# The first three score rows of the next batch, computed in pieces beside the second attention

## The chip, the cores and the metric

One Trainium2 chip, one core of it. The metric is the device time of one execution in microseconds (us); the kernel works on 8 batches one after the other.

## What is computed

The reference, cut to its steps. A batch is 128 channels by 48 x 48 = 2304 positions ("tokens"). All of it is float32.

```
x = x + _L0_conv_ref(_gn(x), ...)          # group norm, then:
#   q, k, v = W x + b;  energy = q^T k  (2304 x 2304);  attn = softmax(energy, rows)
#   gamma * (v attn^T) + x * sigmoid(se_w2 relu(se_w1 mean(x)))
t = _to_tokens(x)
t = t + _L1_attn_ref(_ln_t(t))             # softmax(s s^T) s over 2304 tokens, s = layer norm of t
t = t + _L1_ffn_ref(_ln_t(t), ...)         # 8 experts, the best 2 of each token by router softmax
x = _from_tokens(t, x)
```

## The kernel before

There are no loops on the chip: a list of steps, `PLAN`, is written out, and every engine walks it in order and issues its own part of each step. A step is a tuple such as `("scores", b, n, r, c)`. Each engine is therefore an in-order queue, and semaphores join the queues. Every product is made of three single-pass matmuls of a high and a low part (function `three`, lines 1022 to 1024), so each tensor that goes into one is split first: ScalarE writes the high part, VectorE subtracts it for the low part.

A batch has two attentions.

- **First attention.** It goes in blocks `n` = 0 to 5 of 3 rows of tiles (3 x 128 queries). A stage has 18 slots. In the slots of stage `n`, the scores of block `n` are made (`scores`, 5 chunks for a row: four of 512 columns, one of 256, in PSUM banks 0 to 4), VectorE takes each chunk's maximum (line 840) and the row's (`row_max`, line 844), and ScalarE makes the exponentials into `p_rows` (line 619); the next row's chunks use the same banks, so they wait for these exponentials. In the same slots block `n` - 1 is transposed in 18 pieces (`pt`, line 1036; high part line 631, low part line 850) and multiplied with v (`pv`, into bank 5). Stage 0 has scores alone and stage 6 has `pt` and `pv` of block 5 alone.
- **Second attention.** It has 54 windows `w`. In each, TensorE makes `s1` (six matmuls of 384 columns, banks 0 to 3) and `pv1` of the window two before (six matmuls, banks 4 and 5), ScalarE makes the exponential (line 666) and the high part (line 675), and VectorE the low part (`p1low`, line 924).

Other work is laid beside these windows by tables of window numbers: the statistics, normalisation and q, k, v projections of the next batch (`STATISTICS_SLOTS`, `NORMALISE_SLOTS`, `PROJECT_SLOTS`), the transposes back of the second attention's result (`o1t`, with `o1add`, lines 930 to 938), and the mixture of experts in blocks of 3 tiles (`MOE_SLOTS`, function `moe`): layer norm (`uln`, `uapply`, line 901), transpose (`ut`), `router`, six half products (`expert` for VectorE, line 1005; `scaled` for ScalarE, line 700), GpSimd's sums (lines 519 to 526), and the transpose back `yt`. Of the steps beside a window those named in `SOON` stand ahead of `p1low`. Blocks 4 and 5 of a batch's experts are done beside the second attention of the next batch.

Small results go through a ring of two PSUM banks (6 and 7): each ring step waits until the readers of the step two before have finished (`wait_ring`). Stage 0 of the next batch begins in slots `end` = 54 and up, right behind the last window, beside the last two `pv1`. I call these 18 slots **the turn**; there are seven turns in an execution.

## Time and profile before

| | |
|---|---|
| time, median of 3 runs | 2816.06 us (2815.02 to 2817.49) |
| the profiled execution's own time | 2816.04 us |
| its span in the trace | 2814.3 us |
| TensorE, busy share of the span | 94% |
| VectorE | 77% |
| ScalarE | 72% |
| GpSimd | 16% |

The span runs from the first to the last instruction of the trace; 1.7 us of the profiled time lie outside it. TensorE's busy time is a union of matmuls that overlap and whose ends are modelled, so a busy TensorE is not at its peak, and an idle time that the trace shows before a matmul is a real wait. The granted clock of TensorE is a column of its own.

### The profile page before, as it was taken

Reading aid. Unit: us, or ns where it says so; the run is one execution under the profiler, and the core shown is the slowest. Engines: PE = TensorE matmul, PEld = TensorE weight load, DVE = VectorE, ACT = ScalarE, POOL = GpSimd, SP = SyncE. Lnnn points to the kernel's source line nnn. Section 1 sums busy time; section 2 is a strip of 40 time slices with the busy share of each in tenths; the row PEclk is TensorE's granted clock in tenths of the full one; section 3 lists DMA queues with packets and bytes.
Section 4 is the critical chain, followed back from the end, with each engine's and each line's share of the span. In section 5 each row is a group of like instructions: output and inputs, shape, how many; then the busy total and the mean of one; then the engine's idle time right before and its main releaser. Section 6 shows DMA issues by size and latency. Waiting matters only on the chain.

```text
span 2814.3 us, 45757 instructions
## 1 busy us (share of the span) xinstructions
PE 2638.2 (94%) x15334; PEld 2379.7 (85%) x15334; DVE 2161.1 (77%) x5496; ACT 2027.1 (72%) x4308; POOL 447.5 (16%) x840
## 2 busy tenths in 40 slices
PE   6999999999999999999999999998999999999996
PEld 5889978899788997889888898888988889888895
DVE  6877778777787777877778777787778877788675
ACT  4768767687676876767767687776877778677774
POOL 0000310032101320012300123001220022200223
PEclk9999999999999999999999999999999999999997
DMA  1000000000000000000000000000000000000000
GB/s 36 1 18 1 7 7 1 18 7 9 4 1 18 7 10 4 1 18 7 12 1 1 18 10 9 1 1 21 7 9 1 1 21 7 9 1 1 4 9 12
DMA packets 11320, 23.15 MB, mean 8 GB/s; under 512 B 1360, under 2 KB 7760, under 8 KB 11088
## 3 DMA queue, kind: packets, MB, share of 16 engines
q1 hardware_dynamic: 11088, 20.20, 2.0%
q8 instruction: 127, 2.08, 0.3%
q14 instruction: 105, 0.86, 0.1%
...
## 4 chain that ended last, share of the span: by engine, by line
PE 62%; DVE 23%; ACT 9%; issue 5%; POOL 1%; DMA 0%; ACTq 0%; DVEq 0%; SPq 0%; POOLq 0%
PE ps L1022 18%; PE ps L1024 17%; PE ps L1023 17%; PE ps L1036 9%; DVE mx L840 6%; DVE pt_lo L850 3%; DVE pt_lo L924 3%; ACT pt_hi L631 2%; ACT p_rows L619 2%; DVE u_tok L901 1%; ACT p_rows L666 1%; POOL u_rs L529 1%; ACT pt_hi L675 1%; DVE acc L1005 1%; DVE negmax L844 1%
## 5 line engine op out<-in xcount | busy, mean ns | idle before, releaser
L631 ACT ACTIVATE pt_hi<-ps 128x384 fp32r<-128x384 f32 x864 | 426.3, 493 | 319.4 <-PE ps L1036 314.1
L850 DVE TENSOR_TENSOR pt_lo<-ps,pt_hi 128x384 fp32r<-128x384 f32 x864 | 479.3, 556 | 179.6 <-ACT pt_hi L631 171.6
L619 ACT ACTIVATE p_rows<-ps,negmax 128x512 f32<-128x512 f32 (+1 forms) x720 | 465.5, 648 | 67.2 <-DVE negmax L844 60.4
L924 DVE TENSOR_TENSOR pt_lo<-p_rows,pt_hi 128x768 fp32r<-128x768 f32 x432 | 413.7, 959 | 123.8 <-ACT pt_hi L675 122.0
L840 DVE TENSOR_REDUCE mx<-ps 128x1 f32<-128x512 f32 (+1 forms) x720 | 443.0, 633 | 72.2 <-PE ps L1024 48.5
L1036 PE MATMUL ps<-ident,p_rows 128*128 128x128 f32 x2736 | 456.2, 276 | 43.0 <-DVE pt_lo L850 22.8
L666 ACT ACTIVATE p_rows<-ps,shift 128x768 f32<-128x768 f32 x432 | 389.8, 902 | 118.2 <-PE ps L1024 113.7
L1036 PEld LDWEIGHTS ps<-ident,p_rows 128*128 128x128 f32 x2736 | 331.3, 140 | 159.6 <-issue 60.9
L675 ACT ACTIVATE pt_hi<-p_rows 128x768 fp32r<-128x768 f32 x432 | 365.6, 846 | 39.8 <-PE ps L1024 0.4
L1022 PE MATMUL ps<-pt_hi,v_hi 128*128 128x384 f32 x864 | 358.3, 415 | 2.5 <-ACT y_out L640 2.5
L1022 PE MATMUL ps<-xt_hi 128*128 128x384 f32 x864 | 305.3, 353 | 0.0
L1022 PE MATMUL ps<-pt_hi,tn_hi 128*128 128x384 f32 x864 | 291.8, 338 | 9.6 <-ACT y_out L640 7.6
L1022 PE MATMUL ps<-k_hi,q_hi 128*128 128x512 f32 (+1 forms) x720 | 278.4, 387 | 16.3 <-ACT p_rows L619 16.2
L1024 PE MATMUL ps<-xt_hi,xt_lo 128*128 128x384 f32 x864 | 291.6, 337 | 0.0
L1024 PE MATMUL ps<-pt_hi,v_lo 128*128 128x384 f32 x864 | 291.5, 337 | 0.0
L1023 PE MATMUL ps<-xt_lo,xt_hi 128*128 128x384 f32 x864 | 291.4, 337 | 0.0
L1023 PE MATMUL ps<-pt_lo,v_hi 128*128 128x384 f32 x864 | 290.1, 336 | 0.0
L1024 PE MATMUL ps<-pt_hi,tn_lo 128*128 128x384 f32 x864 | 289.3, 335 | 0.0
L1023 PE MATMUL ps<-pt_lo,tn_hi 128*128 128x384 f32 x864 | 288.9, 334 | 0.0
L1023 PE MATMUL ps<-k_lo,q_hi 128*128 128x512 f32 (+1 forms) x720 | 272.9, 379 | 0.0
L1024 PE MATMUL ps<-k_hi,q_lo 128*128 128x512 f32 (+1 forms) x720 | 271.8, 377 | 0.0
L513 POOL TENSOR_TENSOR ln_rs<-ln_ve,minus_half 128x3 f32<-128x3 f32 x48 | 41.9, 873 | 1302.4 <-DVE ln_ve L888 1302.4
(165 smaller groups left out, 5159.5 us busy)
## 6 DMA issues: line engine op xcount, KB each, us to landing
...
biases<-channel SPq DMA_DIRECT2D x1, 2.0 KB, 4.9
```

Source lines behind the costliest of these rows:

```text
L513: pool.tensor_tensor(ln_rs[:, :], ln_ve[:, :], minus_half[:, :], ALU.pow).then_inc(ln_rstd_ready, 1)
L619: act.activation(p_rows[:, ROW_BUFFER[r, n % 2], a:a + w], ps[:, c, 0:w], ACT.Exp, bias=negmax[:, r % 2:r % 2 + 1], accum_out=dparts[:, n, ...
L631: act.activation(pt_hi[:, slot, :], ring_bank(step)[:, 0:BW], ACT.Copy)\
L666: act.activation(p1_f[:, w % 2, :].rearrange("p (s w) -> p s w", s=2), ps[:, 2 * (w % 2):2 * (w % 2) + 2, 0:BW], ACT.Exp, bias=shift[:, :])\
L675: act.activation(p1_hi[:, w % 3, :], p1_f[:, w % 2, :], ACT.Copy).then_inc(p1_hi_ready, 1)
L840: link(dve.tensor_reduce(mx[:, c:c + 1], ps[:, c, 0:QC[c][1]], AX.X, ALU.max))
L850: dve.tensor_tensor(pt_lo[:, slot, :], ring_bank(step)[:, 0:BW], pt_hi[:, slot, :], ALU.subtract).then_inc(pt_lo_ready, 1)
L924: dve.tensor_tensor(p1_lo[:, w % 3, :], p1_f[:, w % 2, :], p1_hi[:, w % 3, :], ALU.subtract).then_inc(p1_lo_ready, 1)
L1022: pe.matmul(out, lhs_hi, rhs_hi, start=start, stop=False)
L1023: pe.matmul(out, lhs_hi, rhs_lo, start=False, stop=False)
L1024: return pe.matmul(out, lhs_lo, rhs_hi, start=False, stop=stop)
L1036: ins = pe.transpose(ring_bank(step)[:, k * 128:(k + 1) * 128], src(k), ident[:, :])
```

## The change

The scores of block 0 of the next batch (its first three rows, 15 chunks) are no longer made in the turn. They become 15 steps `early`, each in the ring, beside windows 25 to 47 of the second attention. TensorE fills a ring bank with a chunk, ScalarE copies it to `p_rows` in SBUF, VectorE takes its maximum from there (`early`), then the maximum of the row (`early_max`), and ScalarE takes the exponential in place in three pieces of 768 columns (`early_exp`, windows 30 to 53). The turn then starts with stage 1: the scores of block 1 together with `pt` and `pv` of block 0.

With it come: `ROW_BUFFER` and the places of `o1_chan` and `terms` in `p_rows` are exchanged, so that these rows are free; the k, q and v projections, the statistics and the normalisation move to earlier windows; the experts' tables move up, so that the last `yt` stands in window 54 and not 60, each `yt` two windows behind its last `scaled` and no longer three; `uln` and `uapply` of block 4 move into stage 6 of the next batch; and `router` is divided: its last exponential on ScalarE and the operations of VectorE behind it are a step `gates`, one window later.

```diff
-ROW_BUFFER = {(0, 0): 0, (0, 1): 1, (1, 0): 2, (1, 1): 3, (2, 0): 4, (2, 1): 4}
+ROW_BUFFER = {(0, 0): 1, (0, 1): 0, (1, 0): 3, (1, 1): 2, (2, 0): 4, (2, 1): 4}
...
-    if n + 1 < NB and j == 13:
+    if n + 1 < NB and j == 13 and (n or not b):
...
-    if k < 3 and 1 <= row <= NB * TPB:
+    if k < 3 and (TPB + 1 if b else 1) <= row <= NB * TPB:
         s.append(("exp", b, (row - 1) // TPB, (row - 1) % TPB, k + 2))
+    if n == NB and b:
+        s += {7: [("uln", b - 1, 4)], 13: [("uapply", b - 1, 4)]}.get(j, [])
...
-MOE_SLOTS = [(2, 4, range(6, 12), 14), (10, 12, range(15, 21), 23), (21, 23, range(26, 32), 34), (30, 32, range(35, 41), 43),
-             (39, 41, range(44, 50), 52), (47, 49, [52, 53, 54, 55, 56, 57], 60)]
-STATISTICS_SLOTS = [4, 5, 6, 7, 8, 9, 10, 11, 12, 13, 14, 15]
-NORMALISE_SLOTS = [14, 15, 16]
-PROJECT_SLOTS = {15: [("xg", 0)], 16: [("xg", 1)], 17: [("kproj", 0), ("xg", 2)], 19: [("kproj", 1)], 21: [("kproj", 2)],
-                 22: [("kproj", 3)], 23: [("base", 0)], 24: [("kproj", 4)], 25: [("kproj", 5)], 26: [("base", 1)],
-                 28: [("vproj", 0)], 29: [("base", 2)], 31: [("vproj", 1)], 32: [("vproj", 2)], 33: [("vproj", 3)],
-                 41: [("vproj", 4)], 42: [("vproj", 5)], 43: [("qproj", 0)]}
+MOE_SLOTS = [(None, 0, 2, range(4, 10), 11), (6, 10, 11, range(13, 19), 20), (21, 23, 24, range(26, 32), 33),
+             (30, 32, 33, range(35, 41), 42), (39, 41, 42, [43, 44, 44, 45, 45, 46], 48), (44, 47, 48, [50, 50, 51, 51, 52, 52], 54)]
+STATISTICS_SLOTS = [0, 0, 2, 2, 4, 4, 5, 6, 7, 8, 9, 12]
+NORMALISE_SLOTS = [8, 9, 11]
+PROJECT_SLOTS = {10: [("xg", 0)], 11: [("xg", 1)], 12: [("kproj", 0)], 13: [("xg", 2), ("kproj", 1)],
+                 14: [("kproj", 2)], 15: [("kproj", 3)], 16: [("kproj", 4)], 17: [("kproj", 5)], 18: [("qproj", 0), ("base", 0)],
+                 19: [("vproj", 0)], 21: [("vproj", 1)], 22: [("vproj", 2), ("base", 1)], 23: [("vproj", 3)], 24: [("vproj", 4)],
+                 30: [("vproj", 5)], 34: [("base", 2)], 53: [("qproj", 1)]}
+EARLY_SLOTS = [([25, 25, 26, 27, 28], 29, [30, 32, 33]), ([31, 32, 34, 34, 35], 36, [39, 41, 42]),
+               ([39, 40, 43, 46, 47], 48, [49, 51, 53])]
...
+def early(b):
+    s = {}
+    for r, (banks, top, exps) in enumerate(EARLY_SLOTS):
+        for c, slot in enumerate(banks):
+            merge(s, {slot: [("early", b, r, c)]})
+        merge(s, {top: [("early_max", b, r)]})
+        for u, slot in enumerate(exps):
+            merge(s, {slot: [("early_exp", b, r, u)]})
+    return s
...
-SOON = ("expert", "scaled", "kproj", "vproj", "qproj")
+SOON = ("expert", "scaled", "kproj", "vproj", "qproj", "early", "early_max", "gates")
...
-    s = [step for n in range(1, NB + 1) for j in range(NT) for step in attention0(b, n, j)]
+    s = [step for n in range(2 if b else 1, NB + 1) for j in range(NT) for step in attention0(b, n, j)]
...
-        merge(beside, {end + 3: [("o1t", b, 4)], end + 6: [("o1t", b, 5)]})
-        merge(beside, {end + j: attention0(b + 1, 0, j) for j in range(NT)})
-        for m, slot in ((4, end + 4), (5, end + 10)):
-            at = beside[slot].index(("row_max", b + 1, 0, m - 4)) + 1
-            beside[slot].insert(at, ("o1add", b, m))
+        merge(beside, early(b + 1))
+    if b + 1 < B:
+        merge(beside, {end + j: attention0(b + 1, 1, j) for j in range(NT)})
+        merge(beside, {end + 4: [("o1t", b, 4), ("o1add", b, 4)], end + 7: [("o1t", b, 5), ("o1add", b, 5)]})
...
-        o1_chan = p_rows[:, 3, 0:2 * LW].rearrange("p (s w) -> p s w", s=2)
+        o1_chan = [p_rows[:, 2, 0:LW], p_rows[:, 0, 2 * LW:3 * LW]]
...
+                elif kind == "early":
+                    r, c = step[2:]
+                    a, w = QC[c]
+                    act.wait_ge(ring_full, filled(step))
+                    if r == TPB - 1:
+                        act.wait_ge(xg_lo_ready, at(xg_lo_ready, "xg", b, LB - 1))
+                    act.activation(p_rows[:, ROW_BUFFER[r, 0], a:a + w], ring_bank(step)[:, 0:w], ACT.Copy).then_inc(early_copied, 1)
+                elif kind == "early_exp":
+                    r, u = step[2:]
+                    act.wait_ge(early_copied, at(early_copied, "early", b, r, len(QC) - 1))
+                    act.wait_ge(early_max_ready, at(early_max_ready, "early_max", b, r))
+                    row = p_rows[:, ROW_BUFFER[r, 0], u * LW:(u + 1) * LW]
+                    act.activation(row, row, ACT.Exp, bias=early_negmax[:, r:r + 1],
+                                   accum_out=dparts[:, 0, r, u:u + 1]).then_inc(early_exp_ready, 1)
...
-                        act.wait_ge(pv1_done, at(pv1_done, "pv1", b - 1, LB * NT - 1))
+                        act.wait_ge(pv1_done, at(pv1_done, "pv1", b - 1, LB * NT - 3 + j // 2))
...
+                elif kind == "early":
+                    r, c = step[2:]
+                    a, w = QC[c]
+                    dve.wait_ge(early_copied, at(early_copied, *step))
+                    if r and not c:
+                        dve.wait_ge(early_max_ready, at(early_max_ready, "early_max", b, r - 1))
+                    dve.tensor_reduce(early_mx[:, c:c + 1], p_rows[:, ROW_BUFFER[r, 0], a:a + w], AX.X, ALU.max)\
+                        .then_inc(early_ready, 1)
+                elif kind == "early_max":
+                    r = step[2]
+                    dve.wait_ge(early_ready, at(early_ready, "early", b, r, len(QC) - 1))
+                    dve.tensor_reduce(early_negmax[:, r:r + 1], early_mx[:, :], AX.X, ALU.max, negate=True)\
+                        .then_inc(early_max_ready, 1)
                 elif kind == "row_max":
...
+                elif kind == "early":
+                    r, c = step[2:]
+                    if not r and not c:
+                        pe.wait_ge(q_lo_ready, at(q_lo_ready, "qproj", b, 0))
+                        pe.wait_ge(k_lo_ready, at(k_lo_ready, "kproj", b, NB - 1))
+                    wait_ring(step)
+                    a, w = QC[c]
+                    tile = slice(r * 128, (r + 1) * 128)
+                    three(ring_bank(step)[:, 0:w], q_hi[:, 0, tile], q_lo[:, 0, tile], k_hi[:, a:a + w], k_lo[:, a:a + w])\
+                        .then_inc(ring_full, 1)
...
+                    if b and not n:
+                        pe.wait_ge(early_exp_ready, at(early_exp_ready, "early_exp", b, TPB - 1, j // (LW // 128)))
+                    else:
+                        pe.wait_ge(p_rows_ready, at(p_rows_ready, "exp", b, n, TPB - 1, chunk_of(j)))
...
                     link(dve.tensor_scalar(rank[:, :, :], rank[:, :, :], 2.0, None, ALU.is_lt))
-                    dve.wait_ge(vector_chain, chained(step, links[0]))
+                elif kind == "gates":
+                    m = step[2]
+                    shape = [128, TPB, E]
+                    dve.wait_ge(vector_chain, chained(("router", b, m), linked(("router", b, m))))
                     dve.wait_ge(gate_exp_ready, at(gate_exp_ready, *step))
                     link(dve.tensor_tensor(gexp[:, :, :], gexp[:, :, :], rank[:, :, :], ALU.mult))
                     dve.wait_ge(vector_chain, chained(step, links[0]))
```

What it does to the order, at three places of the first batch's end. First TensorE around the turn, before (`ident,acc` is `yt`, `ident,p_rows` in this place `o1t` of the second attention's result, `k_hi,q_hi` scores of block 0):

```order
L1024 MATMUL ps<-ew_hi,u_lo 128x512
L1036 MATMUL ps<-ident,p_rows 128x128 x3
L1022 MATMUL ps<-k_hi,q_hi 128x512
L1023 MATMUL ps<-k_lo,q_hi 128x512
L1024 MATMUL ps<-k_hi,q_lo 128x512
L1022 MATMUL ps<-k_hi,q_hi 128x256
L1023 MATMUL ps<-k_lo,q_hi 128x256
L1024 MATMUL ps<-k_hi,q_lo 128x256
L1036 MATMUL ps<-ident,acc 128x128 x3
L1036 MATMUL ps<-ident,p_rows 128x128 x3
L1022 MATMUL ps<-k_hi,q_hi 128x512
```

The same place after (`ident,p_rows` is now `pt` of block 0, `k_hi,q_hi` scores of block 1, `pt_hi,tn_hi` the last `pv1`):

```order
L1091 MATMUL ps<-ident,acc 128x128 x3
L1091 MATMUL ps<-ident,p_rows 128x128 x3
L1077 MATMUL ps<-k_hi,q_hi 128x512
L1078 MATMUL ps<-k_lo,q_hi 128x512
L1079 MATMUL ps<-k_hi,q_lo 128x512
L1077 MATMUL ps<-pt_hi,tn_hi 128x384
L1078 MATMUL ps<-pt_lo,tn_hi 128x384
L1079 MATMUL ps<-pt_hi,tn_lo 128x384
L1077 MATMUL ps<-pt_hi,tn_hi 128x384
L1078 MATMUL ps<-pt_lo,tn_hi 128x384
L1079 MATMUL ps<-pt_hi,tn_lo 128x384
L1091 MATMUL ps<-ident,p_rows 128x128 x3
```

The experts' products and block 0's scores are gone from the turn, `yt` has moved ahead of the first scores, and a transpose stands beside each chunk. Then ScalarE late in the second attention, before (L666 and L675 are a window's two operations, L700 a `scaled`, L686 the high part of `ut`):

```order
L666 ACTIVATE p_rows<-ps,shift 128x768
L675 ACTIVATE pt_hi<-p_rows 128x768
L700 ACTIVATE p_rows<-ps,gates 128x128 x4
L666 ACTIVATE p_rows<-ps,shift 128x768
L675 ACTIVATE pt_hi<-p_rows 128x768
L666 ACTIVATE p_rows<-ps,shift 128x768
L675 ACTIVATE pt_hi<-p_rows 128x768
L700 ACTIVATE p_rows<-ps,gates 128x128 x4
L686 ACTIVATE u_hi<-ps,plus_one 128x384
```

And after, about the same windows (L700 and L709 are the window's two, L734 a `scaled`, L648 the copy of an `early`, L720 `ut`):

```order
L700 ACTIVATE p_rows<-ps,shift 128x768
L709 ACTIVATE pt_hi<-p_rows 128x768
L734 ACTIVATE p_rows<-ps,gates 128x128 x4
L700 ACTIVATE p_rows<-ps,shift 128x768
L709 ACTIVATE pt_hi<-p_rows 128x768
L734 ACTIVATE p_rows<-ps,gates 128x128 x4
L648 ACTIVATE p_rows<-ps 128x512
L700 ACTIVATE p_rows<-ps,shift 128x768
L709 ACTIVATE pt_hi<-p_rows 128x768
L648 ACTIVATE p_rows<-ps 128x256
L720 ACTIVATE u_hi<-ps,plus_one 128x384
```

Each window now has a `scaled` or a copy, or both, where windows with nothing of their own stood between them. Last VectorE behind the router of block 2, before (the rows start in the middle of the router's chain; L924 is `p1low`, L1005 and L1003 an `expert`):

```order
L971 TENSOR_REDUCE rank<-cmp_gt 128x24
L973 TENSOR_SCALAR rank<-rank 128x24
L976 TENSOR_TENSOR gexp<-gexp,rank 128x24
L978 TENSOR_REDUCE gsum<-gexp 128x3
L980 RECIPROCAL gsum<-gsum 128x3
L982 TENSOR_TENSOR gates<-gexp,gsum 128x24
L924 TENSOR_TENSOR pt_lo<-p_rows,pt_hi 128x768 x2
L1005 SCALAR_TENSOR_TENSOR acc<-ps,gates,t_tok 128x128
L1003 TENSOR_SCALAR p_rows<-ps,gates 128x128
```

And after (L976 is `p1low`, L1060 and L1058 an `expert`, L881 the maximum of a piece):

```order
L1025 TENSOR_SCALAR rank<-rank 128x24
L1031 TENSOR_TENSOR gexp<-gexp,rank 128x24
L1033 TENSOR_REDUCE gsum<-gexp 128x3
L1035 RECIPROCAL gsum<-gsum 128x3
L1037 TENSOR_TENSOR gates<-gexp,gsum 128x24
L1060 SCALAR_TENSOR_TENSOR acc<-ps,gates,t_tok 128x128
L1058 TENSOR_SCALAR p_rows<-ps,gates 128x128
L1060 SCALAR_TENSOR_TENSOR acc<-ps,gates,acc 128x128
L1060 SCALAR_TENSOR_TENSOR p_rows<-ps,gates,p_rows 128x128
L881 TENSOR_REDUCE early_mx<-p_rows 128x1
L976 TENSOR_TENSOR pt_lo<-p_rows,pt_hi 128x768
```

Two `p1low` stood between the gates and the first `expert`; now the `expert` and a maximum of 512 columns stand ahead of the next `p1low`.

## Rows read from the trace of the kernel before

**Rows 1.** The page: busy time of each engine, and granted clock in 40 slices.
```profile
PE 2638.2 (94%) x15334; PEld 2379.7 (85%) x15334; DVE 2161.1 (77%) x5496; ACT 2027.1 (72%) x4308; POOL 447.5 (16%) x840
PEclk9999999999999999999999999999999999999997
```
**Rows 2.** Busy by stretch (length; engines; PEclk, DMA): windows 0-17, 18-35, 36-53; stages 3, 6.
```profile
886.30:940.90 54.60, 49.84 (x282) 46.39 (x281) 44.27 (x129) 41.12 (x66) 16.10 (x24) 1.00 0.01 5
940.90:996.60 55.70, 54.85 (x327) 52.61 (x326) 42.41 (x114) 45.76 (x77) 14.06 (x28) 1.00 0.02 8
996.60:1050.80 54.20, 53.70 (x309) 50.68 (x308) 40.30 (x109) 42.70 (x74) 15.65 (x33) 1.00 0.02 8
1106.50:1134.30 27.80, 26.98 (x166) 23.89 (x165) 23.48 (x57) 20.24 (x54) 0.86 (x1) 1.00 0.00 1
1214.00:1230.80 16.80, 15.00 (x98) 12.91 (x99) 11.21 (x31) 8.26 (x18) 0.85 (x1) 1.00 0.21 72
```
**Rows 3.** The same view of the seven turns: first, second, and the sum.
```profile
362.30:389.70 27.40, 21.55 (x114) 17.53 (x112) 20.49 (x50) 16.23 (x47) 6.38 (x15) 1.00 0.02 8
705.00:735.30 30.30, 24.48 (x114) 19.99 (x112) 20.78 (x50) 16.22 (x47) 6.41 (x15) 0.89 0.02 7
...
sum 204.70, PE 164.13 PEld 133.41 DVE 144.59 ACT 113.76 POOL 44.56; mean PE 23.45 PEld 19.06 DVE 20.66 ACT 16.25 POOL 6.37
```
**Rows 4.** Timeline of TensorE, the third turn (start us, us, ..., idle before).
```profile
1059.93 0.55 PE L1036 MATMUL ps<-ident,acc 128*128 128x128 f32 x3 [2.04 <-POOL acc L526]
...
1062.17 0.63 PE L1024 MATMUL ps<-k_hi,q_lo 128*128 128x512 f32 x1
1062.60 0.63 PE L1022 MATMUL ps<-k_hi,q_hi 128*128 128x512 f32 x1
...
1067.71 0.50 PE L1022 MATMUL ps<-k_hi,q_hi 128*128 128x512 f32 x1 [1.77 <-ACT p_rows L619]
...
1073.67 0.55 PE L1036 MATMUL ps<-ident,p_rows 128*128 128x128 f32 x3 [1.78 <-ACT p_rows L619]
```
**Rows 5.** Timeline of TensorE: two score matmuls of 512 columns back to back.
```profile
1051.02 0.39 PE L1022 MATMUL ps<-k_hi,q_hi 128*128 128x512 f32 x1
1051.25 0.39 PE L1023 MATMUL ps<-k_lo,q_hi 128*128 128x512 f32 x1
```
**Rows 6.** The chain of a last `scaled`: TensorE's last matmul, GpSimd's last sum.
```profile
982.70 0.40 PE L1024 MATMUL ps<-ew_hi,u_lo 128*128 128x512 f32 x1
...
986.24 0.46 POOL L526 TENSOR_TENSOR acc<-acc,p_rows 128x128 f32<-128x128 f32 x1
```
**Rows 7.** Waits of TensorE, windows 0-17: total, times, longest us.
```profile
PE ps L1036 <- DVE u_tok L901: 2.8, 2, 1.7
PE ps L1022 <- ACT y_out L640: 0.9, 1, 0.9
```
**Rows 8.** Timeline of VectorE: `uln` and `uapply` of one block.
```profile
1238.56 0.67 DVE L881 BATCH_NORM_STATS2 u_raw<-t_late 128x6 f32<-128x128 f32 x3
...
1239.61 0.17 DVE L888 TENSOR_SCALAR u_ve<-u_mv 128x3 f32<-128x3 f32 x1
...
1241.93 0.86 DVE L901 TENSOR_SCALAR u_tok<-t_late,u_mv,u_rs 128x128 f32<-128x128 f32 x3
```
**Rows 9.** Waits of TensorE, 1203 to 1232 us (around stage 6).
```profile
PE ps L1036 <- DVE pt_lo L850: 1.9, 5, 0.6
```
**Rows 10.** Groups by form, 886.3 to 1232.2 us: count, busy us, mean ns, idle before.
```profile
L631 ACT ACTIVATE pt_hi<-ps 128x384 fp32r<-128x384 f32 x108 | 53.3, 494 | 39.6 <-PE ps L1036 39.0
L840 DVE TENSOR_REDUCE mx<-ps 128x1 f32<-128x512 f32 x72 | 49.3, 687 | 9.4 <-PE ps L1024 6.3
L675 ACT ACTIVATE pt_hi<-p_rows 128x768 fp32r<-128x768 f32 x55 | 46.5, 846 | 5.0
L619 ACT ACTIVATION_READ_ACCUMULATOR p_rows<-ps,negmax 128x1 f32 x90 | 18.6, 207 | 0.0
L682 ACT ACTIVATE p_rows<-ps 128x768 f32<-128x768 f32 x3 | 2.4, 799 | 0.6 <-PE ps L1024 0.6
```

More of the change, by code:

```diff
@@ L95, in normalise, with moe @@
     return [("xgnorm", b, u) for u in range(LB)]
-def moe(b, m, norm, ut, experts, out):
-    s = {norm: [("uln", b, m)], norm + 1: [("uapply", b, m)], ut: [("ut", b, m)], ut + 1: [("router", b, m)], out: [("yt", b, m)]}
+def moe(b, m, norm, ut, router, experts, out):
+    s = {ut: [("ut", b, m)], router: [("router", b, m)], router + 1: [("gates", b, m)], out: [("yt", b, m)]}
+    if norm is not None:
+        merge(s, {norm: [("uln", b, m)], norm + 1: [("uapply", b, m)]})
     for i, slot in enumerate(experts):
@@ L149, in batch @@
     if b + 1 < B:
-        merge(beside, {slot: [step] for slot, step in zip(STATISTICS_SLOTS, statistics(b + 1))})
+        for slot, step in zip(STATISTICS_SLOTS, statistics(b + 1)):
+            merge(beside, {slot: [step]})
         merge(beside, {slot: [step] for slot, step in zip(NORMALISE_SLOTS, normalise(b + 1))})
         merge(beside, {slot: [(step[0], b + 1, step[1]) for step in steps] for slot, steps in PROJECT_SLOTS.items()})
+    for m, slot in enumerate([20, 29, 38, 41]):
+        merge(beside, {slot: [("o1t", b, m), ("o1add", b, m)]})
     blocks = [(b - 1, m) for m in (4, 5)] + [(b, m) for m in range(4)]
@@ L171, in batch @@
             s.append(("s1", b, w))
-        if w == end + LAG - 1:
-            s += beside[w]
         if LAG <= w < end + LAG:
@@ L177, in batch @@
                 s.append(("o1evac", b, (w - LAG) // NT))
-        if w != end + LAG - 1:
-            steps = beside.get(w, [])
-            first = [step for step in steps if step[0] in SOON and w < end - LAG]
-            s += first
-            if w < end:
-                s.append(("p1low", b, w))
-            s += [step for step in steps if step not in first]
+        steps = beside.get(w, [])
+        first = [step for step in steps if step[0] in SOON and w < end - LAG]
+        s += first
+        if w < end:
+            s.append(("p1low", b, w))
+        s += [step for step in steps if step not in first]
     return s
@@ L214 @@
         "yt": "y_chan_ready"}
-CHAINED = {"stat": 1, "gn_dev": 2, "se_out": 6, "rowsum": 3, "ot": 2, "ln": 6, "o1add": 5, "uln": 6, "router": 11,
+CHAINED = {"stat": 1, "gn_dev": 2, "se_out": 6, "rowsum": 3, "ot": 2, "ln": 6, "o1add": 5, "uln": 6, "router": 8, "gates": 3,
            "expert": 3, "scores": 1, "lnapply": 2, "uapply": 2}
@@ L853, in take @@
                     m = step[2]
-                    dve.wait_ge(p_rows_ready, at(p_rows_ready, "exp", b, m, TPB - 1, len(QC) - 1))
-                    link(dve.tensor_reduce(rg[:, 0, :], dparts[:, m, :, :], AX.X, ALU.add))
+                    if b and not m:
+                        dve.wait_ge(early_exp_ready, at(early_exp_ready, "early_exp", b, TPB - 1, LB - 1))
+                        parts = dparts[:, m, :, 0:LB]
+                    else:
+                        dve.wait_ge(p_rows_ready, at(p_rows_ready, "exp", b, m, TPB - 1, len(QC) - 1))
+                        parts = dparts[:, m, :, :]
+                    link(dve.tensor_reduce(rg[:, 0, :], parts, AX.X, ALU.add))
                     dve.wait_ge(vector_chain, chained(step, links[0]))
@@ L1106, in take @@
                     row = n * TPB + r
-                    if row:
+                    if row > (TPB if b else 0):
                         pe.wait_ge(p_rows_ready, at(p_rows_ready, "exp", b, (row - 1) // TPB, (row - 1) % TPB, c))
```

43 lines of the change are left out of this document (23 added, 20 removed).

## The prediction

> **What bounds the kernel now.** I read the page first: TensorE is busy 94% of the span, VectorE 77%, ScalarE 72%, and the granted clock is at nine tenths or more in all slices but the last [rows 1]. So a gain can only come from stretches in which TensorE waits or runs slow, and the next view is its busy time by stretch. One batch takes about 345 us. In a full stage of the first attention (stage 3) it idles 27.80 - 26.98 = 0.82 us; in windows 18 to 35 it idles 0.85 us of 55.70, in windows 36 to 53 0.50 us of 54.20 [rows 2]. There nothing is to be had. Idle time sits in three other places: the turn, windows 0 to 17 (54.60 - 49.84 = 4.8 us), and stage 6 (16.80 - 15.00 = 1.8 us) [rows 2, 3]. The seven turns take 204.70 us together, and TensorE is busy in 164.13 of them: 40.6 us idle, 5.8 each [rows 3].
>
> The timeline of one turn says why. TensorE first waits 2.04 us for GpSimd's last sum, which `yt` transposes, and then twice 1.8 us for exponentials: a row's chunks are made in about 3 us, but the next row needs the same banks, and VectorE's maxima and ScalarE's exponentials stand between [rows 4]. Nothing else is queued that could fill these waits. The clock suffers too: after the 2.04 us two matmuls of 512 columns stand 1062.60 - 1062.17 = 0.43 us apart, against 1051.25 - 1051.02 = 0.23 us before it [rows 4, 5]; that is the 1.2 GHz level against the 2.4. The first turn ran at a granted clock of 1.00 in 27.4 us, the second at 0.89 in 30.3 [rows 3].
>
> **The change part by part.** The sum is per execution, against the profiled 2816.0 us, which is the median of the runs too.
>
> *The turn.* In its place stands a stage that has both scores and transposes, like stage 3. Such a stage idles 0.82 us, so 40.6 - 7 x 0.82 = 34.8 us of idle time go. With the long wait goes the slow clock: 204.7 - 7 x 27.4 = 12.9 us. Together **-47.7 us**.
>
> *The score matmuls themselves* gain nothing. A row is 4.5 chunks of 512 columns with three matmuls each at 0.23 us [rows 5], 3.1 us, three rows 9.3 us per batch; they leave the turn and lengthen the windows by the same, because TensorE is the one that is full there. The six half products, projections and `yt` that change places count nothing for the same reason.
>
> *The new `yt` wait.* The last `scaled` now stands in window 52, `yt` in 54 ahead of the first scores. From the start of a last matmul of such a product to the end of GpSimd's last sum I read 986.24 + 0.46 - 982.70 = 4.0 us [rows 6]. TensorE has behind it one `s1`, two `pv1` (18 matmuls of 384 columns, 0.17 each by the 512-column spacing, 3.1 us) and `qproj` (0.5), 3.6 us, plus the last matmul's own 0.23. So it waits a little; at least 0, at most today's 2.04. I take 0.7, nearer to the sum of the two rows: **+4.9 us**.
>
> *Windows 0 to 17.* 2.8 of the 4.8 us idle are two waits for `u_tok`, the normalised block of the experts [rows 7]. Block 4's now comes from stage 6 and block 5's has four windows in place of two. Against that, VectorE is at 44.27 of 54.60 us there [rows 2], its statistics come in pairs in windows 0, 2 and 4, and k projections move in. Between 0 and -2.8; I take -1.5, seven times: **-10.5 us**. The 0.9 us wait for the first `pv1` [rows 7] stays.
>
> *Stage 6* gets this `uln` and `uapply`: (1239.61 + 0.17 - 1238.56) + 0.86 = 2.1 us of VectorE [rows 8], in a stretch where TensorE already waits 1.9 us in five pieces for `pt_lo` [rows 9], though VectorE is busy only 11.21 of 16.80 us [rows 2]. Between 0 and 2.1; I take 0.7, since two thirds can go into VectorE's pauses: **+4.9 us**.
>
> *The denser windows*, the term that decides. Per batch ScalarE gets 15 copies and 9 exponentials. No row shows a copy of 512 columns from PSUM: 384 columns take 0.494 us, 768 take 0.799 [rows 10]; I take 0.6. A 768-column operation on SBUF takes 0.846 [rows 10], with its accumulator read (0.207) 1.05. For windows 36 to 53: 42.7 us today [rows 2], + 5 copies 3.0, + 6 exponentials 6.3, + two `scaled` and a `yt` from the turn (about 2.8), - two v projections 1.0 = 53.8 us. TensorE's time there grows by 5 chunks (one short) 3.1, four half products 2.8, `yt` 0.3, less two v projections 2.0: 54.2 + 4.3 = 58.5 us. ScalarE goes from 79% to 92%, and it must be in time in every window, for both the next `s1` and the ring. In windows 18 to 35 the same count gives 45.8 + 10 copies 5.7 + 3 exponentials 3.2, about 53.5 of 62 us, 86%. VectorE gets 15 maxima; from PSUM one takes 0.687 [rows 10], hence some 9 us per batch, and it stays at about 80%, but each waits at the head of its queue for a copy, with `p1low` and so `pv1` behind it, and behind block 2's router the `expert` now stands ahead of `p1low`. The nearest rows give bounds: from nothing, as the idle of 0.50 us at 79% suggests, to both stretches idling like windows 0 to 17, where VectorE is at 81% in bursts: 2 x 4.8 - 0.85 - 0.50 = 8.2 us. I take 3.0, nearer to the low end because operands are two windows ahead: **+21 us**.
>
> One rule weighs on this. The Trainium skill, "VectorE: DVE Perf Modes", section "Rules for kernel authors", advises to copy a PSUM result to SBUF first only if many operations follow; here one maximum and one exponential do. By its cost table (section on the TRN2 errata) a 512-column maximum would cost about 0.59 us from SBUF and 0.66 from PSUM, so by that rule the copies buy VectorE 1 us per batch for some 8.6 us more of ScalarE, and the change should lose wherever ScalarE is full. The row for the maximum from PSUM is 0.687, near its figure. It is the mechanism of the slower rival below.
>
> Sum: 2816.0 - 47.7 + 4.9 - 10.5 + 4.9 + 21 = **2788.6 us**, 1.0% less.
>
> **The rivals.** *All of it* (0.20): dense windows cost nothing, both `u_tok` waits go: 2816.0 - 47.7 - 19.6 + 4.9 = 2754 us, to 2768 with small costs. For it: 18 windows with ScalarE at 79 to 82% cost TensorE under 1 us of idle now. Against it: 92% is a different load.
>
> *The turn still waits* (0.10): `yt` waits 2 us for GpSimd and the clock falls again. Then 12.9 us of clock stay lost and the wait costs 1.3 us more in each of seven turns: 2788.6 + 12.9 + 9.1 = 2811 us, no measurable change. For it: the gap between `scaled` and `yt` shrinks by a window. Against it: these windows last 3 us and more, the slots of the turn 1.5.
>
> *ScalarE becomes the bound* (0.12): the windows wait for it. At 8.2 us per batch, the upper bound above: 2788.6 + 7 x 5.2 = 2825 us, slower. It decides from (2816.0 - 2788.6) / 7 + 3.0 = 6.9 us per batch on. For it: 92%, and no second queue to go to. Against it: in steady stages ScalarE waits for TensorE, not the reverse (39.6 us before `pt_hi`) [rows 10].
>
> My forecast has 0.58, with a range of its own of 2768 to 2806.
>
> **How the numbers follow.** About 0.2% (5.6 us) is what a measurement of this kernel tells from no change. Faster: 0.58 + 0.20 and a small part of the other two, 0.80. Slower: 0.09 of ScalarE's 0.12, and 0.01 of the turn's. Same: the rest, 0.10. Leaving one in ten out on either side gives 2757 to 2812.
>
> **What would show it.** Right: between the last window and stage 2 TensorE idles under 2 us, granted clock 1.00 in all turns; the waits for `u_tok` near zero early; the new maximum about 0.6 us; windows 18 to 53 with 2 to 4 us more of idle, ended by ScalarE's outputs or by a ring bank. Wrong: matmuls of 384 columns waiting for exponentials in every dense window, or waits of 1 us and more in windows 25 to 53 that add up to 7 us per batch; `yt` waiting 2 us for GpSimd with a clock under 1.00; stage 6 longer by 2 us.

## The result, and the profile after the change

The changed kernel takes 2803.0 us (median of 5 runs, 2801.34 to 2805.84); the kernel before takes 2815.35 beside it (2815.02 to 2817.49). The ratio is 0.9955, with an interval of 0.9941 to 0.9970: 12.4 us or 0.44% faster. I had forecast 27.4 us. The span of the profiled execution fell from 2814.3 to 2801.6 us. The page of the changed kernel, busy times and granted clock, reads almost like [rows 1]; only ScalarE has more, 74% in place of 72%:

```profile
PE 2630.3 (94%) x15334; PEld 2372.1 (85%) x15334; DVE 2158.9 (77%) x5496; ACT 2070.6 (74%) x4329; POOL 467.8 (17%) x840
PEclk9999999999999999999999999999999999999997
```

So the answer lies in the stretches. Busy time by stretch of the changed kernel, columns as in [rows 2]: windows 0 to 17, 18 to 35, 36 to 53, what is left of the turn (to the start of stage 2), stage 3, stage 6, and this whole batch:

```profile
1225.10:1282.20 57.10, 53.79 (x301) 49.82 (x300) 46.99 (x129) 44.59 (x75) 16.11 (x28) 1.00 0.01 4
1282.20:1344.80 62.60, 60.07 (x359) 56.91 (x358) 44.89 (x117) 51.65 (x86) 12.07 (x22) 1.00 0.02 7
1344.80:1403.00 58.20, 55.81 (x307) 51.42 (x305) 44.08 (x120) 49.61 (x94) 23.01 (x45) 1.00 0.02 8
1403.00:1428.90 25.90, 23.53 (x140) 20.09 (x141) 18.81 (x42) 16.24 (x39) 1.81 (x3) 1.00 0.02 9
1454.50:1482.30 27.80, 27.00 (x167) 23.89 (x165) 23.47 (x57) 20.26 (x54) 0.85 (x1) 1.00 0.00 1
1549.90:1567.60 17.70, 15.14 (x99) 12.96 (x98) 13.16 (x42) 8.26 (x17) 1.70 (x2) 1.00 0.19 67
1225.10:1567.60 342.50, 325.93 (x1917) 294.42 (x1916) 268.80 (x686) 258.86 (x541) 58.11 (x103) 1.00 0.02 8
```

TensorE idles 2.4 us in the turn, not 5.8 [rows 3]. But windows 18 to 35 now idle 62.60 - 60.07 = 2.5 us and windows 36 to 53 idle 2.4, where they idled 0.85 and 0.50 [rows 2]. Most of the idle time has not gone; it has moved from the turn into the windows.

To see this over the whole execution I took, for each stretch of every batch, its length less the issue time of its matmuls (0.232 us for 512 columns, 0.174 for 384, 0.117 for 256, 0.110 for 128, the spacings in the trace). I call the rest **slack**: idle time and slow clock together. The sums over the batches, in us:

| stretch | before | after | difference | forecast |
|---|---|---|---|---|
| the turn (with the `yt` wait) | 63.8 | 28.0 | -35.8 | -42.8 |
| windows 0 to 17 | 53.4 | 44.3 | -9.1 | -10.5 |
| windows 18 to 53 | 37.2 | 63.4 | +26.2 | +21 |
| stages 2 to 5 | 43.0 | 44.2 | +1.2 | 0 |
| stage 6 | 31.7 | 36.4 | +4.7 | +4.9 |

They sum to -12.8 us. The wait of 0.44 us before the projection of window 53 (below) stands in the row of the turn here, while the line of windows 36 to 53 above still holds it. Idle time alone fell by 22.2 us in the turn and rose by 22.0 in windows 18 to 53. What the kernel kept goes mainly with the clock: before, nine stretches in the turns ran at a low granted clock; after the change three do, all in the dense windows, one of them here:

```profile
1700.00:1712.00 12.00, 10.14 (x53) 9.51 (x52) 9.17 (x26) 9.48 (x18) 3.75 (x6) 0.86 0.00 0
```

Where the new idle time comes from is best seen around window 41. The timeline of the changed kernel; first TensorE, and below it VectorE, ScalarE and GpSimd in the 5 us before:

```profile
1363.88 0.55 PE L1091 MATMUL ps<-ident,u_tok 128*128 128x128 f32 x3 [1.84 <-DVE u_tok L953]
```
```profile
1360.97 0.69 DVE L881 TENSOR_REDUCE early_mx<-p_rows 128x1 f32<-128x512 f32 x1 [1.47 <-ACT p_rows L648]
1361.57 1.07 DVE L976 TENSOR_TENSOR pt_lo<-p_rows,pt_hi 128x768 fp32r<-128x768 f32 x1
1362.56 1.26 DVE L953 TENSOR_SCALAR u_tok<-t_tok,u_mv,u_rs 128x128 f32<-128x128 f32 x3
```
```profile
1358.57 0.85 ACT L709 ACTIVATE pt_hi<-p_rows 128x768 fp32r<-128x768 f32 x1
1359.32 1.12 ACT L734 ACTIVATE p_rows<-ps,gates 128x128 f32<-128x128 f32 x4
1360.32 0.61 ACT L648 ACTIVATE p_rows<-ps 128x512 f32<-128x512 f32 x1
```
```profile
1361.78 1.17 POOL L548 TENSOR_TENSOR p_rows<-p_rows 128x128 f32<-128x128 f32 x1
```

Read from the bottom up: ScalarE makes an exponential, a `scaled` and then the copy, which ends at 1360.93. VectorE has stood 1.47 us for it with the maximum at the head of its queue. Behind the maximum are the low part of the window and `uapply`, which took 1.26 us while GpSimd was adding. TensorE waits 1.84 us for its result `u_tok`. The waits of the whole execution (total, times, longest us) name the same pair:

```profile
DVE early_mx L881 <- ACT p_rows L648: 46.1, 42, 2.3
...
PE ps L1091 <- DVE u_tok L953: 34.6, 19, 6.4
```

And in the turn, `yt` waits 0.18 us now and not 2.04 [rows 4], but behind it a transpose waits for the merge `o1add` (it writes `t_late`), which holds a bank of the ring; 6 us later another does, 0.78 us. The timeline of TensorE there:

```profile
1402.95 0.41 PE L1077 MATMUL ps<-xg_hi,w_hi 128*128 128x384 f32 x1 [0.44 <-DVE p_rows L1060]
1404.94 0.55 PE L1091 MATMUL ps<-ident,acc 128*128 128x128 f32 x3 [0.18 <-POOL acc L550]
1413.25 0.52 PE L1091 MATMUL ps<-ident,p_rows 128*128 128x128 f32 x3 [0.44 <-DVE pt_lo L897]
1415.03 0.52 PE L1091 MATMUL ps<-ident,p_rows 128*128 128x128 f32 x3 [0.74 <-DVE t_late L990]
```

### The profile page after: what moved, and what is told of

Its sections match the earlier page's. It is cut to its first block, busy times and chain, and to the rows that moved or that the text cites. A ratio compares the mean times of both kernels' runs of the same rounds, so it can differ in the third digit from the quotient of the medians.

```text
span 2801.6 us, 45883 instructions
## 1 busy us (share of the span) xinstructions
PE 2630.3 (94%) x15334; PEld 2372.1 (85%) x15334; DVE 2158.9 (77%) x5496; ACT 2070.6 (74%) x4329; POOL 467.8 (17%) x840
## 4 chain that ended last, share of the span: by engine, by line
PE 62%; DVE 20%; ACT 10%; issue 6%; POOL 2%; DMA 0%; ACTq 0%; SPq 0%; DVEq 0%; POOLq 0%
PE ps L1077 18%; PE ps L1079 17%; PE ps L1078 17%; PE ps L1091 8%; DVE mx L874 5%; DVE pt_lo L897 4%; ACT pt_hi L665 3%; ACT p_rows L639 2%; DVE pt_lo L976 2%; ACT p_rows L700 1%; ACT p_rows L734 1%; DVE u_tok L953 1%; ACT pt_hi L709 1%; PE ps L1256 1%; PE ps L1257 1%
## 5 line engine op out<-in xcount | busy, mean ns | idle before, releaser
L976 DVE TENSOR_TENSOR pt_lo<-p_rows,pt_hi 128x768 fp32r<-128x768 f32 x432 | 417.2, 966 | 134.9 <-ACT pt_hi L709 133.5
L700 ACT ACTIVATE p_rows<-ps,shift 128x768 f32<-128x768 f32 x432 | 390.7, 904 | 163.8 <-PE ps L1079 151.0
L639 ACT ACTIVATE p_rows<-ps,negmax 128x512 f32<-128x512 f32 x615 | 398.5, 648 | 20.6 <-DVE negmax L891 14.3
L874 DVE TENSOR_REDUCE mx<-ps 128x1 f32<-128x512 f32 x615 | 378.8, 633 | 45.2 <-PE ps L1079 21.9
L709 ACT ACTIVATE pt_hi<-p_rows 128x768 fp32r<-128x768 f32 x432 | 365.6, 846 | 40.7 <-PE ps L1079 1.1
L1077 PE MATMUL ps<-k_hi,q_hi 128*128 128x512 f32 (+1 forms) x720 | 270.8, 376 | 3.9 <-ACT p_rows L639 3.8
```

Of the source, the lines that this page charges most:

```text
L639: act.activation(p_rows[:, ROW_BUFFER[r, n % 2], a:a + w], ps[:, c, 0:w], ACT.Exp, bias=negmax[:, r % 2:r % 2 + 1], accum_out=dparts[:, n, ...
L700: act.activation(p1_f[:, w % 2, :].rearrange("p (s w) -> p s w", s=2), ps[:, 2 * (w % 2):2 * (w % 2) + 2, 0:BW], ACT.Exp, bias=shift[:, :])\
L709: act.activation(p1_hi[:, w % 3, :], p1_f[:, w % 2, :], ACT.Copy).then_inc(p1_hi_ready, 1)
L874: link(dve.tensor_reduce(mx[:, c:c + 1], ps[:, c, 0:QC[c][1]], AX.X, ALU.max))
L976: dve.tensor_tensor(p1_lo[:, w % 3, :], p1_f[:, w % 2, :], p1_hi[:, w % 3, :], ALU.subtract).then_inc(p1_lo_ready, 1)
L1077: pe.matmul(out, lhs_hi, rhs_hi, start=start, stop=False)
```

## The experiments

The theories, by the letters that the expectations use. For the dense windows: **A**, VectorE's queue stands for a copy that ScalarE has not made yet, and `uapply` and so `ut` behind it come late; **B**, ScalarE's load itself; **C**, VectorE's load. For the turn: **D**, `o1add` keeps a ring bank too long, and its rival, that the turn is not set by it.

Ratios are against the kernel before, run beside each on the same chip (2814.5, 2815.0 and 2817.2 us in the three groups, e1 to e4, e5 to e8, and the last three).

| kernel | us, median of 4 | ratio | interval |
|---|---|---|---|
| e1_late_max | 2791.9 | 0.9915 | 0.9900 to 0.9930 |
| e2_short_exp | 2798.7 | 0.9939 | 0.9924 to 0.9954 |
| e3_short_max | 2793.0 | 0.9924 | 0.9909 to 0.9939 |
| e4_turn_order | 2804.1 | 0.9955 | 0.9938 to 0.9971 |
| e5_o1t_behind | 2785.3 | 0.9893 | 0.9879 to 0.9908 |
| e6_statistics | 2798.0 | 0.9933 | 0.9917 to 0.9950 |
| e7_stage6_back | 2826.8 | 1.0044 | 1.0029 to 1.0059 |
| e8_short_add | 2777.0 | 0.9869 | 0.9855 to 0.9884 |
| e10_late_short_exp | 2782.4 | 0.9882 | 0.9867 to 0.9897 |
| f1_o1t_40 | 2781.6 | 0.9879 | 0.9864 to 0.9894 |
| f2_o1t_40_turn | 2779.1 | 0.9869 | 0.9853 to 0.9885 |

An interval is some 4 us to either side, so a smaller difference between two kernels rests on their traces. The traces are of one execution each, and these differ where no experiment touches them: the start, up to the scores of the first batch's block 1, takes 44 us in some and 49 in others.

### Each maximum one window after its copy

```diff
             merge(s, {slot: [("early", b, r, c)]})
+            merge(s, {slot + 1: [("early_in", b, r, c)]})
...
-                elif kind == "early":
+                elif kind == "early_in":
                     r, c = step[2:]
```

The new step stands ahead of `p1low`, as `early` did.

> The changed kernel with each piece's maximum one window after its copy, so that VectorE never stands at the head of its queue for ScalarE's copy; nothing else is moved. Theory A (the dense windows cost 26 us because VectorE waits for the copies, 46.1 us in 42 waits, with the uapply behind them, and the transpose of u_tok on TensorE then waits): those waits fall under 5 us, the two waits for u_tok (1.2 and 1.8 us per batch) shrink by more than half, and the kernel takes 2785 to 2795 us against 2803. Theory B (ScalarE's load): 2801 to 2805, waits for u_tok stay. Theory C (VectorE's load, the maxima themselves): 2801 to 2805.

11.1 us less than the changed kernel; in the traces windows 18 to 53 lose 13.0 us of slack (50.4, was 63.4), and no other stretch changes by much more than 1. No wait of VectorE for a copy is left, and 14 of the 19 waits for `u_tok` are gone (compare the two lines in the section on the result); the five left are in the last batch, which has no `early`. The waits of TensorE in this kernel:

```profile
PE ps L1092 <- DVE u_tok L954: 13.5, 5, 6.4
...
PE ps L1092 <- DVE t_tok L991: 8.4, 8, 1.2
```

Not one operation became shorter or fewer. Around window 41 this shows theory A by itself: a maximum, that of the copy one window before, still stands ahead of the low part and `uapply`, but nothing waits for a copy. VectorE there:

```profile
1352.07 0.69 DVE L882 TENSOR_REDUCE early_mx<-p_rows 128x1 f32<-128x512 f32 x1
1353.06 0.96 DVE L977 TENSOR_TENSOR pt_lo<-p_rows,pt_hi 128x768 fp32r<-128x768 f32 x1 [0.30 <-ACT pt_hi L710]
1353.93 1.17 DVE L954 TENSOR_SCALAR u_tok<-t_tok,u_mv,u_rs 128x128 f32<-128x128 f32 x3
```

At window 32, where the other wait for `u_tok` stood (1.18 us), the edit also took the maximum itself, 0.69 us, from ahead of `uapply`; there A and C are not told apart. Of the two lines on TensorE the second is new: the wait has moved on to window 42, where a transpose needs the ring bank that `o1add` of window 41 still reads. It is 1.1 to 1.2 us long, and in four of seven batches the clock falls behind it, in three not. Here one of each, 11 us around window 42:

```profile
1016.00:1027.00 11.00, 9.87 (x48) 8.87 (x47) 7.64 (x26) 7.47 (x13) 0.00 (x0) 0.84 0.06 20
674.00:685.00 11.00, 9.84 (x57) 8.96 (x56) 9.04 (x27) 9.04 (x16) 0.46 (x1) 1.00 0.06 19
```

With the fall, windows 42 to 47 have 3.4 us of slack, without it 1.8: a fall costs 1.6 us.

### Less work for ScalarE, less work for VectorE

e2 makes the early exponentials over 8 columns of each 768; e3 takes the early maxima over 8 of each 512.

```diff
-                    row = p_rows[:, ROW_BUFFER[r, 0], u * LW:(u + 1) * LW]
+                    row = p_rows[:, ROW_BUFFER[r, 0], u * LW:u * LW + 8]
```
```diff
-dve.tensor_reduce(early_mx[:, c:c + 1], p_rows[:, ROW_BUFFER[r, 0], a:a + w], AX.X
+dve.tensor_reduce(early_mx[:, c:c + 1], p_rows[:, ROW_BUFFER[r, 0], a:a + 8], AX.X
```

> The changed kernel with the nine early exponentials of a batch cut from 768 to 8 columns (so the exponentials of block 0's rows are left out but for 8 columns of each piece): some 0.7 us of ScalarE less for each, 6 us per batch. Theory B: the windows' idle falls by 10 us and more in all, time 2785 to 2793. Theory A: only copies that stand behind an exponential come sooner, 2799 to 2803. Theory C: 2801 to 2804.

> The changed kernel with the fifteen maxima of a batch taken over 8 columns of each piece in place of 512 or 256 (the rest of each piece is left out of the maximum): some 0.5 us of VectorE less for each, 8 us per batch; each still waits for its copy. Theory C: the windows' idle falls by 10 us and more, 2785 to 2793. Theory A: the wait for the copy stays and only 0.5 us behind it goes, 2795 to 2801. Theory B: 2801 to 2804.

e2: 4.3 us less, just under the range of A and well above that of B; the wait for copies hardly changed (43.8 us). In its trace the idle time of windows 36 to 53 is 5 us less and that of windows 18 to 35 the same. ScalarE's load has a share, but it is not what makes VectorE wait. e3: 10 us less, the time that C gives (its profiled execution took 2799.1 us, the other three 2792.5 to 2793.2). But the trace shows that VectorE did not become free: it only reached the next copy sooner and stood longer for it:

```profile
DVE early_mx L881 <- ACT p_rows L648: 57.8, 49, 2.8
```

What is late is the queue, wait and work together, so shortening either helps. That fits e3 and e1 giving nearly the same time. The time alone would not have told A from C; e1, which takes no work away, does at window 41.

### The same delay, with the short exponentials

e1 and e2 together.

> The late maximum (2791.9 us) and the nine early exponentials of a batch cut to 8 columns of each piece (the others are left out): the ScalarE work that is taken away is the same 6 us per batch that gave 4.3 us when VectorE still stood waiting for the copies. Theory A (ScalarE's load costs only through the copies that VectorE waits for): 2789 to 2793 us. Theory B (its load costs by itself): 2783 to 2788.

9.5 us less than e1 (9.3 by the ratios), 0.6 under the range of theory B and far from that of A. So with the waits for copies gone, ScalarE's load still costs nearly as much as they did. The trace shows by which way. The wait for `t_tok` fell only from 8.4 to 7.5 us in all, but none of e1's four falls of the clock is left (4 x 1.6 = 6.4 us). The stretch around window 42 in this kernel:

```profile
1010.00:1036.00 26.00, 24.98 (x142) 23.32 (x141) 21.66 (x59) 20.92 (x44) 12.70 (x22) 1.00 0.03 9
```

About 3 us, 9.5 - 6.4, are left for everything but the clock (idle time is 4 us less in windows 18 to 53 and 1.5 more in the turn). The rest is clock that was there again when seven waits of 1.13 us shrank to about 1.0. That the shorter wait is the reason isn't shown: behind seven waits of 1.1 us at this place the clock fell four times in e1 and in e6, twice in e8 and once in e7.

### The merge later, or earlier by a window

e5 puts `o1t` and `o1add` behind the experts' steps of the same window; f1 has that, and the merge of window 41 in window 40. Both stand on e1.

```diff
-    for m, slot in enumerate([20, 29, 38, 41]):
-        merge(beside, {slot: [("o1t", b, m), ("o1add", b, m)]})
     blocks = [(b - 1, m) for m in (4, 5)] + [(b, m) for m in range(4)]
     for (c, m), slots in zip(blocks, MOE_SLOTS):
         if c >= 0:
             merge(beside, moe(c, m, *slots))
+    for m, slot in enumerate([20, 29, 38, 41]):
+        merge(beside, {slot: [("o1t", b, m), ("o1add", b, m)]})
```

> On top of the late maximum (2791.9 us): in windows 20, 29, 38 and 41, o1t and o1add stand behind the experts' steps of the window, not ahead of them. In the trace with the late maximum TensorE waits 1.1 to 1.2 us, 8.4 us in 8 waits, at yt of window 42 for the o1add of window 41, and in the later of two such waits in one look the granted clock fell to 0.84. Theory A (what is left in the dense windows is ring order, an o1add of 2 us in a bank with too little behind it): those waits go, 2780 to 2787 us. Theory B (ScalarE's load): no change, 2789 to 2794.

> The late maximum, o1t behind the experts' steps (2785.3 us), and the o1t and o1add of block 3 in window 40 and no longer in 41. In windows 42 to 47 there is still one wait of 1.2 us for o1add, now at the router, and in most batches 1.6 us more behind it in which the granted clock is low. Theory A (ring order): both go, 2770 to 2780 us. Rival H (VectorE has no room for 2 us in windows 39 to 41, and block 2's u_tok comes late instead): 2784 to 2790.

e5: 6.6 us less than e1 (6.2 by the ratios), the size that I had expected, but partly at another place: the waits of the v projections for `t_tok` in windows 18 to 23 (5.1 us) are gone; the one at window 42 stayed and now stands before the router:

```profile
PE ps L1257 <- DVE t_tok L991: 8.9, 8, 1.2
```

f1: another 3.7 us. The wait for `t_tok` is gone, but two others grew in its place, from 6.2 and 0 us in e1:

```profile
PE ps L1078 <- DVE p_rows L1061: 9.9, 16, 2.0
...
PE ps L1092 <- ACT p_rows L735: 6.8, 7, 1.0
```

The time lies between the two ranges. By idle time f1 is slightly worse than e5, by 2 us in windows 18 to 53. Its gain is that these waits are shorter each and no low clock is left in the windows, where e5 has four falls.

### The order of the turn, and a short merge

e4 puts the two merges of the turn right behind `pt` of their slot. e8, on e1, takes `o1add` of blocks 4 and 5 over 8 of 128 columns in six of the seven turns, and leaves the other sums out.

```diff
-        merge(beside, {end + 4: [("o1t", b, 4), ("o1add", b, 4)], end + 7: [("o1t", b, 5), ("o1add", b, 5)]})
+        for m, slot in ((4, end + 4), (5, end + 7)):
+            behind = beside[slot].index(("pt", b + 1, 0, slot - end)) + 1
+            beside[slot][behind:behind] = [("o1t", b, m), ("o1add", b, m)]
```
```diff
+                    cut = 8 if m >= 4 and 0 < b < B - 1 else 128
```

> The changed kernel with the two last o1t and o1add placed right behind pt in their slots of the turn, ahead of pv and the scores chunk, so that TensorE has two slots of other work before the transpose that needs their ring bank again. Theory D (the turn idles 2.6 us and not 0.8 because o1add, 2 us of VectorE in a ring bank, is covered by one slot of 1.6 us only): the waits of 0.74 and 0.78 us for t_late go, 2792 to 2797 us in place of 2803. Rival E (VectorE is too full in the turn, and what o1add no longer delays is delayed by the row's maximum): the waits move to exponentials or pt_lo and the time stays at 2801 to 2806.

> On top of the late maximum: o1add of blocks 4 and 5 over 8 columns of each tile in place of 128 in six of the seven turns (the rest of these sums is left out), some 1.0 us of VectorE less for each and so a ring bank given back sooner. Theory D (o1add is what makes the turn idle 2.6 us): the waits of 0.74 and 0.78 us for t_late go in six turns, 2782 to 2786 us. Rival E (the turn's stage has other limits that take over, as when the order was changed): 2788 to 2793.

e4 changed nothing that its time shows (2804.1 against 2803.0, the result that rival E gave): the waits for `t_late` halved from 10.7 to 5.2 us, and a wait of 0.55 us for `pt_lo` before another transpose took most of the place; 1.6 us less slack are left in the turns. e8: 14.9 us less than e1 (13 by the ratios), more than D gave. The waits for `t_late` of the changed kernel, and those of e8, of which the two left stand in the turn that was not changed:

```profile
PE ps L1091 <- DVE t_late L990: 10.7, 14, 0.8
```
```profile
PE ps L1093 <- DVE t_late L992: 1.5, 2, 0.8
```

The turn's slack fell from 28 to 19 us, 1.5 in each of the six turns changed. The rest is not the turn's: in the trace 3.2 us are two falls of the clock fewer at window 42, behind waits as long as e1's, and 1.6 lie in the start. The turn of the changed kernel, and that of e8, over the same steps:

```profile
1404.90:1428.90 24.00, 21.78 (x131) 18.65 (x132) 17.47 (x41) 14.56 (x37) 0.00 (x0) 1.00 0.03 9
```
```profile
1391.25:1413.75 22.50, 21.76 (x131) 18.65 (x132) 16.08 (x41) 14.44 (x37) 0.00 (x0) 1.00 0.03 10
```

So D holds in this: `o1add` costs the turn 1.5 us, and its place in the queue hardly matters. It holds its bank for about 2 us where a slot of the turn covers 1.55. But e8 shortens the hold and takes 1.4 us of VectorE's work from the turn (17.47 - 16.08) in one edit, and in e4 the wait moved to `pt_lo`, another of VectorE's results; whether the bank or VectorE's work sets the time is not told apart.

### The early windows

e6, on e1, spreads the statistics; e7, on e1, puts `uln` and `uapply` of block 4 back from stage 6 into windows 0 and 1, and its `ut`, router and products one window later.

```diff
-STATISTICS_SLOTS = [0, 0, 2, 2, 4, 4, 5, 6, 7, 8, 9, 12]
-NORMALISE_SLOTS = [8, 9, 11]
+STATISTICS_SLOTS = [0, 0, 2, 2, 4, 4, 5, 7, 8, 9, 10, 12]
+NORMALISE_SLOTS = [9, 10, 11]
```
```diff
-    if n == NB and b:
-        s += {7: [("uln", b - 1, 4)], 13: [("uapply", b - 1, 4)]}.get(j, [])
...
-MOE_SLOTS = [(None, 0, 2, range(4, 10), 11),
+MOE_SLOTS = [(0, 2, 3, range(5, 11), 12),
```

> On top of the late maximum: the statistics' matrix product gn_dev and the three steps behind it one window later, normalisation one later, and ut of block 5 one window earlier (windows 7 and 9 in place of 6 and 10). Windows 6 to 11 hold 3.5 us more than the issue of their matmuls, of it a wait of 1.25 us for gn_mv and one of 0.8 us for u_lo in each of six batches. Theory F (these are waits of order, from steps packed one window apart): both go, 2780 to 2786 us. Rival G (VectorE is simply full in windows 0 to 11, so the wait moves to pt_lo or another step): 2789 to 2794.

> On top of the late maximum: uln and uapply of block 4 back from stage 6 to windows 0 and 1, with its ut in 2, router in 3, half products 5 to 10 and yt in 12. Prices that move. By the prediction's terms stage 6 gives back 4.7 us and windows 0 to 17 lose what the move had brought (up to 12 us, the u_tok wait of 1.7 us in each of seven batches, less what the other edits brought there): 2790 to 2800 us. Rival: the move brought nothing and only costs stage 6, 2785 to 2789.

e6 became 6 us slower than e1, outside both ranges: the waits that it aimed at are gone (1.2 and 0.8 us in a batch), and two statistics products now wait for a ring bank, 1.7 us in window 8 for an `expert` that reads it and 0.5 in window 12 for a router. The idle time of windows 0 to 17 is 1.6 us less than in e1; what made the kernel slower is the clock, which fell behind the wait of 1.7 us in four of six batches, about 1.5 us each. e7 became 35 us slower, far outside both ranges. Stage 6 gave back what was forecast for it, 4.9 us, but windows 0 to 17 lost 44, of it 28 us idle time and the rest mostly slow clock, with ten falls. Their waits in one batch of e7:

```profile
PE ps L1090 <- DVE k_lo L856: 2.2, 1, 2.2
PE ps L1102 <- DVE gn_mv L777: 1.9, 1, 1.9
PE ps L1255 <- DVE u_lo L996: 1.5, 2, 1.1
PE ps L1090 <- DVE u_tok L952: 1.3, 1, 1.3
```

The changed kernel's own early windows thus depend on how block 4 is placed: bringing it back cost 6.3 us a batch. Not all of this is the 2.1 us of VectorE work that returned. The longest wait, 2.2 us for `k_lo`, is that of `yt`, now in window 12, for the ring bank of a k projection, and comes from the later steps.

### The best full version

f2 is f1 with e4's order of the turn.

> The kernel above, with o1t and o1add of the turn right behind pt. By the one run in which this order stood alone, no change that can be measured: within 3 us of the kernel above. Theory D in its first form would give 5 to 10 us less.

2779.1 us, 2.5 less than f1, as expected: 1.3% faster than the kernel before and 0.9% faster than the change. The turns have 1.7 us less slack than in f1, as in e4. Its page has the same number of instructions on every engine as the changed kernel's; only their order is another:

```profile
PE 2621.6 (94%) x15334; PEld 2366.5 (85%) x15334; DVE 2153.5 (78%) x5496; ACT 2067.0 (74%) x4329; POOL 460.3 (17%) x840
```

## Why the prediction was right in direction and off in size

The measured time lies in the range, and the change is faster, as forecast. But the gain is 12.4 us where 27.4 were forecast. Two terms of the sum failed: the turn, priced as a stage like stage 3, and the dense windows, whose price was no more than a share of a bound. By the table of slack above, the missing part is 7.0 us in the turn, 5.2 in the dense windows, 1.4 in windows 0 to 17 and 1.2 in stages 2 to 5.

**The turn** (forecast -47.7 and +4.9). The step that failed is "In its place stands a stage that has both scores and transposes, like stage 3. Such a stage idles 0.82 us". Stage 3 itself still idles 0.80 us (27.80 - 27.00). What replaced the turn idles 2.4, because it is not stage 3: two merges are in it, and each keeps a ring bank about 2 us. The waits for them are 10.7 us over seven turns, and e8 measured 1.5 us a turn; I had costed them at nothing because their instructions were not new. The sign that I had named for the turn, idle time under 2 us, did not come. The other parts of the term held: the exponentials are no longer waited for, and the granted clock in the turns is 1.00. The new `yt` wait was taken as 0.7 us and is 0.18, which gives back 3.6 us, with 0.44 before a projection ahead of it, 3 us.

**The dense windows** (forecast +21, in the trace +26.2). Idle time alone rose by 22.0, so the size of the term came out, but by luck: 3.0 us a batch was a point between two bounds, and the two waits for `u_tok` happen to be 1.18 + 1.84 us. The other 4 us are slack beyond idle time, and the three falls of the clock in these windows were not in the sum. I had weighed ScalarE's 92% and 86%; it came to 49.61 / 58.20 = 85% and 51.65 / 62.60 = 83%. One reason is that I added whole durations, while neighbours overlap: the `scaled` above ends at 1360.44, and the copy behind it starts at 1360.32. The 86% was also added wrongly: 45.8 + 5.7 + 3.2 is 54.7 us, not 53.5. VectorE, which I put at about 80%, was at 76% and 74% in these windows and came to 72% and 76%.

By the slack of the traces e1 took half of the 26.2 us away, 13.0, e5 another 6 (a wait that the earlier v projections had brought) and f1 another 3. ScalarE's load has its share too, 9.5 us by e10, of which the clock's part is also what f1 got. The half that e1 took is the clause in which I wrote that each maximum "waits at the head of its queue for a copy". I had named `pv1` as what is queued behind it; it was `uapply`, and so `ut`. That clause deserved the term, and a look at which steps stand behind each maximum in these windows would have found the place. The forecast "because operands are two windows ahead" is true of `pv1` alone.

**Windows 0 to 17** (-10.5, in the trace -9.1) and **stage 6** (+4.9, in the trace +4.7) came out as forecast. e7 suggests that the first is a thinner claim than it looked, a balance of what the packed tables cost and what the move to stage 6 saves, both several times larger; but e7 also moved block 4's later steps. The waits left there in one batch are four short ones, none for `u_tok`, and the 0.9 us before the first `pv1` stayed as said:

```profile
PE ps L1103 <- DVE gn_mv L778: 1.2, 1, 1.2
PE ps L1077 <- ACT y_out L674: 0.9, 1, 0.9
PE ps L1256 <- DVE u_lo L997: 0.8, 1, 0.8
PE ps L1077 <- DVE pt_lo L976: 0.3, 1, 0.3
```

**The costs of single operations** were near. Groups by form of one batch of the changed kernel, columns as in [rows 10]:

```profile
L654 ACT ACTIVATE p_rows<-p_rows,early_negmax 128x768 f32<-128x768 f32 x9 | 8.4, 930 | 0.0
...
L881 DVE TENSOR_REDUCE early_mx<-p_rows 128x1 f32<-128x512 f32 x12 | 8.0, 681 | 6.0 <-ACT p_rows L648 6.0
...
L648 ACT ACTIVATE p_rows<-ps 128x512 f32<-128x512 f32 x12 | 7.1, 599 | 1.7 <-PE ps L1079 1.7
```

The copy takes 0.599 us (0.6 taken), the exponential 0.930 (0.846 taken). The maximum takes 0.681 from SBUF against 0.687 from PSUM [rows 10]: moving it to SBUF saved VectorE nothing. The Trainium skill, "VectorE: DVE Perf Modes", section "Rules for kernel authors", advises the copy only where many operations follow, and the trace agrees with the advice; the 0.59 us that its cost table gives for the SBUF form is not seen here.

**The rivals.** *The turn still waits* is out: `yt` waits 0.18 us and the clock stays up. *ScalarE becomes the bound* is out as worded; but the dense windows cost 26.2 / 7 = 3.7 us per batch, over half of the 6.9 from which the change would have lost, and ScalarE's load is part of it (e10). *All of it* did not come.

**Left open.** Whether the bank's hold or VectorE's work sets the turn, and how much of the wait at window 32 is the maximum itself. And when a wait makes the clock fall. In e1 waits of 1.13 and 1.16 us at the same place in the program ended one with a fall and one without, and I found nothing in the trace that tells the two apart.
